# Layer 2 of a graph network: rows picked by TensorE for one column in eight, one chunk at a time, or in batches of four columns with a bfloat16 one-hot matrix

## What is computed

```python
k = (feats @ Wk + bk).reshape(n, H, D)
v = (feats @ Wv + bv).reshape(n, H, D)
score = jnp.sum(k[src] * q[dst], axis=-1)
score = jnp.exp(jnp.clip(score / SCALE, -5.0, 5.0))
wv = jax.ops.segment_sum(v[src] * score[..., None], dst, num_segments=n)
z = jax.ops.segment_sum(score, dst, num_segments=n)
wv = wv / (z[..., None] + 1.0)
```

## Time and profile before

| what | us |
|---|---|
| median of 3 runs | 6179.44 |
| lowest and highest | 6165.42, 6182.65 |
| span of the profiled execution | 5335.3 |
| median less span | 844.1 |
| busy in the span: DVE, POOL, PE, ACT | 3848.7, 3702.3, 3329.0, 2006.2 |
| edge stage of layer 2, first gather to last scan's start | 3097.36 to 4045.84 |

### The profile page before, as it was taken

How to read it: one execution, slowest core, us unless ns; L and a number is a source line. 1 busy time by engine, 2 the same in 40 slices (tenths; PEclk the granted TensorE clock), 3 DMA queues, 4 the chain that set the end, 5 groups by cost and what they waited for, 6 DMA issues and landing times. The chain is left out here.

```text
span 5335.3 us, 59849 instructions
## 1 busy us (share of the span) xinstructions
PE 3329.0 (62%) x17449; PEld 2791.6 (52%) x17449; DVE 3848.7 (72%) x5210; ACT 2006.2 (38%) x3469; POOL 3702.3 (69%) x3472
## 2 busy tenths in 40 slices
PE   1777777753999999999999467777674700000001
PEld 0444444432888889988888467666673500000001
DVE  3888888874999999999999569999996522222223
ACT  0666666641344444444444223333332311111111
POOL 4777777764788888888887356766774077777774
PEclk8899999986999999999999679999996955555555
DMA  7777777764888888888887333333332922222221
GB/s 292 247 267 255 262 264 263 257 214 146 309 319 319 319 321 321 320 320 321 320 321 282 89 92 110 108 108 108 109 108 64 382 52 55 53 54 53 54 56 43
DMA packets 390718, 1060.91 MB, mean 199 GB/s; under 512 B 138843, under 2 KB 161943, under 8 KB 349241
## 3 DMA queue, kind: packets, MB, share of 16 engines
q1 hardware_dynamic: 229430, 755.21, 37.7%
q0 software_dynamic: 104704, 161.21, 12.0%
q10 hardware_dynamic: 56448, 142.93, 7.1%
HBM read 667.35 MB, written 391.75 MB: 199 GB/s over the span
## 5 line engine op out<-in xcount | busy, mean ns | idle before, releaser
L1458 PE MATMUL COLS<-CF,XF 128*128 128x256 f32 x6272 | 1485.4, 380 | 5.6 <-DVE XF L1566 5.6
L1458 PEld LDWEIGHTS COLS<-CF,XF 128*128 128x128 f32 x6272 | 1134.6, 190 | 129.3 <-DVE XF L1566 6.0
L909 ACT ACTIVATE OUT<-SC 128x576 f32<-128x576 f32 (+3 forms) x392 | 574.9, 1467 | 1346.3 <-DVE SC L846 989.8
L784 POOL DMA_INDIRECT G<-rel_tab,IDX_rel x784 | 739.6, 943 | 390.5 <-issue 249.1
L1425 POOL DMA_INDIRECT G<-x_tab,SRC x784 | 833.2, 1063 | 231.5 <-issue 219.2
L784 POOL DMA_INDIRECT G<-xl_tab,IDX_src x784 | 749.7, 956 | 275.0 <-issue 264.4
L784 POOL DMA_INDIRECT G<-kv_tab,IDX_src x686 | 647.1, 943 | 298.3 <-issue 221.6
L1785 PE MATMUL CP<-IDENT,LROW 128*68 128x128 f32 (+1 forms) x12 | 3.4, 422 | 1049.9 <-DVE SM L1906 1049.9
L838 DVE TENSOR_TENSOR MSG<-G,EW 128x512 f32<-128x512 f32 x98 | 100.0, 1020 | 733.3 <-DMA G<-rel_tab,IDX_rel 724.7
L1785 PEld LDWEIGHTS CP<-IDENT,LROW 128*68 128x68 f32 (+1 forms) x12 | 1.5, 157 | 1051.3 <-DVE SM L1906 1051.2
L1196 PE MATMUL PICK<-KV,HOT 125*128 125x128 f32 x2548 | 364.3, 309 | 204.6 <-ACT G L1215 202.5
(11 more groups left out here) (274 smaller groups left out, 6907.6 us busy)
## 6 DMA issues: line engine op xcount, KB each, us to landing
SHB<-ea9t SPq DMA_DIRECT2D x196, 1024.0 KB
wkv_tab<-WKV SPq DMA_DIRECT2D x98, 1024.0 KB
WKV<-wkv_tab SPq DMA_DIRECT2D x98, 1024.0 KB, 5.9
scan<-OUT ACTq DMA_DIRECT2D x196, 288.0 KB
scan<-OUT ACTq DMA_DIRECT2D x98, 576.0 KB
rel_tab<-YS SPq DMA_DIRECT2D x25, 2048.0 KB, 7.3
RAW<-spread SPq DMA_DIRECT2D x196, 256.0 KB
spread_q<-ZQ SPq DMA_DIRECT2D x98, 512.0 KB, 5.3
```

Of the source, the lines that this page charges most:

```text
L784: pool.indirect_dma_start(out=self.G[g][b][:, c, :], out_offset=None, in_=tab, in_offset=bass.IndirectOffsetOnAxis(ap=self.IDX[which][b][: ...
L909: nc.scalar.activation(self.OUT[b][:, :, 0:WD], SC[b][:, 0:WD, 1:1 + C].rearrange("p r j -> p j r"), ACT.Copy).then_inc(self.copied_out, 1)
L1458: nc.tensor.matmul(acc, XF[b][:, k, edges_], CF[:, k, :], start=(k == 0), stop=False)
```

## The change

Layer 2 alone changes. Chunks 0 and 1 are gathered whole. From chunk 2 on, three chunks form a group in which TensorE picks 1, 1 and 2 columns (`picks`), so POOL gathers 7, 7 and 6, and the four picked columns are one batch of 512 edges. There are 32 batches.

- The source numbers of a batch come from the host already in a row (`src4`). SP loads them spread over all partitions into SRC4, ACT narrows them to 16 bits (ID16).
- DVE compares them in 25 instructions for a batch, one for each k: `tensor_scalar` with the partition's node number NODE_F[:, k] as scalar, 512 columns of uint16 in, bfloat16 out, into HOT, which is doubled. The 25 are cut into bursts of 6, 6, 6 and 7 and placed between ARG and MSG of each chunk, and one burst behind the scan.
- The table stays in SBUF as three bfloat16 pieces whose sum is the float32 value (KV3), made in the projection: ACT makes the first piece from TAB, DVE subtracts it (REST), ACT makes the second, DVE subtracts again into the third.
- PE multiplies with the roles turned round: KV3 is the weight and HOT the moving operand, 3 x 25 matmuls of 512 columns for a batch into PICK. The result is transposed, so ACT copies it out (`take`, TURNED), PE transposes it back in four parts (BACK) and ACT places the columns into G (`place`).
- KV's load at the start of the stage, the index loads of each chunk, SPREAD and SRC_F are gone; POOL takes its indices from SRC, which is loaded once. POOL's and DVE's chunks are written out.

```diff
+PICK_FROM = 2
+BATCHES = (NCH - PICK_FROM) // 3
+def picks(t):
+    return 0 if t < PICK_FROM else 2 if (t - PICK_FROM) % 3 == 2 else 1
...
+                        if pieces is not None:
+                            act.wait_ge(m_copied, len(units))
+                            nc.scalar.activation(KV3[:, :, 0, :], TAB[:, :, 0:128], ACT.Copy).then_inc(kv_high, 1)
...
+                                if pieces is not None and g == 1:
+                                    act.wait_ge(kv_rest, 1)
+                                    nc.scalar.activation(KV3[:, :, 1, :], REST[:, :, :], ACT.Copy).then_inc(kv_middle, 1)
...
+                            v.wait_ge(kv_high, 1)
+                            nc.vector.tensor_tensor(REST[:, :, :], TAB[:, :, 0:128], KV3[:, :, 0, :], ALU.subtract)\
+                              .then_inc(kv_rest, 1)
...
+                                if pieces is not None and g == 2:
+                                    v.wait_ge(kv_middle, 1)
+                                    nc.vector.tensor_tensor(KV3[:, :, 2, :], REST[:, :, :], KV3[:, :, 1, :],
+                                                            ALU.subtract).then_inc(kv_low, 1)
...
                     @block.gpsimd
-                        e.gathers(pool)
+                        wait(pool, src_in, 16)
+                        def step(t, n, b, first, last):
+                            wait(pool, e.scanned, t - 1)
+                            for c in range(C - picks(t)):
+                                pool.indirect_dma_start(
+                                    out=e.G[0][b][:, c, :], out_offset=None, in_=kv_tab,
+                                    in_offset=bass.IndirectOffsetOnAxis(ap=SRC[:, t * C + c:t * C + c + 1], axis=0),
+                                ).then_inc(e.rows_in[0][b], 16)
+                        all_chunks(step)
...
                     @block.tensor
+                        for i in range(BATCHES):
+                            wait(pe, compared, 4 * i + 4)
+                            wait(pe, taken, i)
+                            for piece in range(3):
+                                for k in range(K):
+                                    ins = nc.tensor.matmul(PICK[:, :], KV3[N, k, piece, :], HOT[i % 2][N, k, :],
+                                                           start=(piece == 0 and k == 0), stop=(piece == 2 and k == K - 1))
+                            ins.then_inc(picked, 1)
+                            wait(pe, taken, i + 1)
+                            wait(pe, placed, 3 * i)
+                            for q in range(4):
+                                ins = nc.tensor.transpose(BACK[:, q * P:(q + 1) * P], TURNED[:, q * P:(q + 1) * P],
+                                                          IDENT[:, :])
+                            ins.then_inc(turned_back, 1)
...
                     @block.scalar
+                        def narrow(i):
+                            wait(act, src4_in[i % 2], (i // 2 + 1) * 16)
+                            wait(act, compared, 4 * (i - 1))
+                            nc.scalar.activation(ID16[i % 2][:, :], SRC4[i % 2][:, :], ACT.Copy).then_inc(narrowed, 1)
+                        def take(i):
+                            wait(act, picked, i + 1)
+                            wait(act, turned_back, i)
+                            nc.scalar.activation(TURNED[:, :], PICK[:, :], ACT.Copy).then_inc(taken, 1)
...
                     @block.vector
+                        def compare(i, q):
+                            wait(v, narrowed, i + 1)
+                            wait(v, picked, i - 1)
+                            for k in range(6 * q, 6 * q + 6 if q < 3 else K):
+                                ins = nc.vector.tensor_scalar(HOT[i % 2][N, k, :], ID16[i % 2][N, :], NODE_F[N, k:k + 1],
+                                                              None, ALU.is_equal)
+                            ins.then_inc(compared, 1)
...
                         def step(t, n, b, first, last):
+                            if t < PICK_FROM:
+                                ahead = [(1, 2 * t), (1, 2 * t + 1)]
+                            else:
+                                i, r = divmod(t - PICK_FROM, 3)
+                                ahead = [(i + 2, q) for q in ((0, 1), (2,), (3,))[r] if i + 2 < BATCHES]
                             e.expand(v, t, n, b, first)
...
                             scores(t, n, b, first)
-                            if more:
-                                compare(t + 2, 0)
+                            if ahead:
+                                compare(*ahead[0])
                             e.sums(v, t, n, b, first, e.G[0][b][:, :, 64:128])
-                            if more:
-                                compare(t + 2, 1)
-                        chunks(v, step)
+                            if ahead[1:]:
+                                compare(*ahead[1])
+                        all_chunks(step)
```

More of the change, by code:

```diff
@@ L781, in step @@
                     pool.sem_inc(parked, 1)
-                    for c in range(self.gathered):
+                    for c in range(C):
                         for g, (tab, _, which) in enumerate(self.tables):
@@ L1210, in _ @@
+                        narrow(0)
+                        narrow(1)
                         wait(act, e.ready, e.N_READY)
-                        def place(t, b):
-                            wait(act, picked, t + 1)
-                            wait(act, e.scanned, t - 1)
-                            nc.scalar.activation(e.G[0][b][:, C - 1, :], PICK[:, 0:128], ACT.Copy).then_inc(placed, 1)
                         def step(t, n, b, first, last):
```

134 lines of the change are left out of this document (63 added, 71 removed).

## The result

| | before | changed |
|---|---|---|
| median, us | 6172.4 (6162.6 to 6182.7, 4 runs) | 5917.1 (5889.2 to 5942.1, 4 runs) |
| span of the profiled execution | 5335.3 | 5887.5, of a run of 5889.2 |
| ratio of the times | | 0.9587, 95% interval 0.9553 to 0.9622 |

The kernel became 255 us faster. The prediction had 82 us, 6097, with a range of 6058 to 6210: right in sign, wrong in size, and the time fell out of the range. One execution of an experiment stands apart, for a reason that is not known: 13670 us at a granted clock of 0.52, where the nine others of that kernel (before, with PE in a loop) on that chip took 5332 to 5342.

The account below looks back on a forecast made before the run. POOL's gathers were to bound layer 2's edge stage at 26.25 us per three chunks, saving 85 us; less 3 for the projection, 5335.3 - 82 + 844.1 = 6097 us, range 6058 to 6210.

Parts of the forecast that it names:

- what lies around it: Time outside the profiled span: 844.1 us, taken as unchanged and added to the forecast.
- The low end of my range: POOL's floor in layer 2: comparisons near XI's cost, no wait or hold, 24.98 us a period, 6058 us.
- something unseen: Catch-all case, sharing a chance of 0.04 with PE being late.
- The sum itself: Whole kernel: 85 us off layer 2's edge stage, less 3 for the projection, so 82 us off.
- POOL bounds the stage: Layer 2 edge stage: 20 gathers, 24.98 us, set the three-chunk period; 26.25 us with scan wait and holds.
- The hold by the shared access: Layer 2: comparisons delay POOL gather starts by about 0.1 us a burst, 0.4 us in three chunks.
- shut-out rival: Layer 2: gathers stand still while comparisons run, even mid-gather; 6258 or 6209 us; chance 0.13.
- burst-hold rival: Layer 2: a gather waits for its whole burst, 0.6 to 0.8 us each; 6152 us; chance 0.14.
- The wait for the scan: Layer 2: POOL waits 0.87 us for DVE's scan once in three chunks, after a six-gather chunk.
- The projection: Ahead of layer 2's edge stage: added ACT copies and DVE subtractions cost 3 us, bounds 0 and 13.6.
- rival of 1.2 GHz throughout: Layer 2: PE stays at 1.2 GHz, 31 us a batch; 6313 us; within 0.04 for PE late or something unseen.
- ACT's cover: Layer 2: ACT's extra work, under 1 us a chunk, fits its 3.2 us a chunk of waiting for ARG.

Follow-up runs that it names:

- b_unlinked_2: Kernel before with nobody waiting for TensorE in layer 2, its 25 matmuls a chunk kept; late chip: 6344.4 us beside 6169.2 for before.
- a_unlinked_2: Changed kernel with batch matmuls kept but their result untaken (no transposes, takes or placements); late chip: 5894.8 us beside 6169.2 for before.

## Why the prediction was wrong, step by step

**The step that failed** is the term "what lies around it, 6179.4 - 5335.3 = 844.1 by the median (830 to 847 by the three runs), I leave as it is". Of a timed run under 3 us lie around its span. The profile was of an execution without late starts (on quick chips before takes 5332 to 5346 us), the timed runs were on chips with them. Of the 255 us, 106 are what the change saves on a quick chip. The other 149 are late time that it happened to take away, 109 to 143 of them in layer 2 by the stages' lengths: that stage is 305 us longer on a late chip with the kernel before, and 162 to 196 with the changed one. The low end of my range, 6058, carried the same constant, and so could not hold the time. The prediction named it under what would make it wrong ("if the time around the span moves") but gave it no chance of its own beyond the 0.04 for "something unseen"; a difference of 16% between span and time deserved a rival. That the error fell on the side of the gain is luck: no term of the sum knew of late time.

Part of the mechanism of the extra gain is shown. In the kernel before each chunk has DVE wait for PE's spread and for PICK, so that each late start of PE goes through DVE's row, 280 us of waiting in 47 pieces, to POOL. In the changed kernel DVE's comparisons wait for the batch two before. That a kernel with nobody waiting for PE had a stage of 978 us shows that this link carried 256 of the 305. In the changed kernel another of the prediction's signs of being wrong came up on late chips: ACT does wait for PICK (132.9 us in 18 times), and through it DVE. But taking that link away left 989 us, so it is not what bounds the stage there; DVE's late scans are a part of it (76.4 of the 149 us that are left). Why engines start late at all stays open.

**The sum itself**, 85 us from the stage, less 3, measured on a quick chip: 102 us from the stage and 4 outside it, so 24 too few. One period of three chunks there, DVE, the rows that answer to the earlier trace rows (the last one begins the next period):

```profile
3498.24 1.90 DVE L1292 TENSOR_SCALAR HOT<-ID,NODE_F 125x512 bf16<-125x512 uint16 x6
3500.06 1.02 DVE L867 TENSOR_TENSOR MSG<-G,XE 128x512 f32<-128x512 f32 x1
...
3505.78 2.10 DVE L1292 TENSOR_SCALAR HOT<-ID,NODE_F 125x512 bf16<-125x512 uint16 x7
3507.80 1.03 DVE L867 TENSOR_TENSOR MSG<-G,XE 128x512 f32<-128x512 f32 x1
...
3512.99 0.69 DVE L1306 TENSOR_TENSOR T<-G,XE 128x512 f32<-128x512 f32 x1 [1.04 <-DMA G<-kv_tab,SRC]
...
3514.52 1.93 DVE L1292 TENSOR_SCALAR HOT<-ID,NODE_F 125x512 bf16<-125x512 uint16 x6
3516.37 1.03 DVE L867 TENSOR_TENSOR MSG<-G,XE 128x512 f32<-128x512 f32 x1
...
3518.90 1.82 DVE L1292 TENSOR_SCALAR HOT<-ID,NODE_F 125x512 bf16<-125x512 uint16 x6
3520.64 0.22 DVE L800 COPY XI<-XE 128x64 f32<-128x64 f32 x1
...
3523.83 1.89 DVE L1292 TENSOR_SCALAR HOT<-ID,NODE_F 125x512 bf16<-125x512 uint16 x6
```

and POOL's gathers in that stage (group), its one wait in three chunks, and the last gather, which answer to the earlier trace rows:

```profile
L1223 POOL DMA_INDIRECT G<-kv_tab,SRC x654 | 618.8, 946 | 220.3 <-issue 193.1 <-DVE SC L885 27.2
```
```profile
3501.06 0.94 POOL L1223 DMA_INDIRECT G<-kv_tab,SRC  x1 [0.30 <-issue]
3502.82 0.94 POOL L1223 DMA_INDIRECT G<-kv_tab,SRC  x1 [0.81 <-DVE SC L885]
...
3937.60 0.94 POOL L1223 DMA_INDIRECT G<-kv_tab,SRC  x1 [0.30 <-issue]
```

- *DVE.* The bursts take 1.82, 2.02, 1.85 and 1.74 us, together 7.43 against my 6.25: 0.30 a comparison, not 0.25. Undisturbed they start 0.26 apart, so the pitch itself was nearly right; the rest is that gathers hold them, some 0.85 us a period (763 comparisons last 0.380 on average, the median 0.346). The rest of three chunks takes 17.1 (25.59 less 7.43 and the idle 1.04) against 17.28. DVE needs 24.6 us where I had 23.5; the 31.9 us period of the double comparison (17.1 + 14.9) agrees. DVE keeps one spare microsecond in a period. I had left out that gathers hold comparisons, and it is hidden anyway.
- *POOL bounds the stage*: right. From the first gather's start to the last one's it is 840.4 us: less the first 20 and with one pitch of 1.25 added, 25.7 us a period, against 26.25.
- *The hold by the shared access*, 0.4 us a period on POOL: not there. The mean gather is 946 ns. Only three of the 640 behind the first 20 us took over 970. The shut-out rival and the burst-hold rival, 0.27 of the chance together, are both refuted, by the group row above and by the double comparison. The hold is on the other engine, as above: a comparison in a gather's middle lasts 0.53 us instead of 0.35. The rule of the Trainium skill on the shared port (SBUF — State Buffer, SBUF: two separate sides) has both sides: of a DVE instruction of certain kinds and a GpSimd one, whichever starts first keeps the other out for its whole length. These rows agree in so far as a gather makes a comparison wait. They do not in that a comparison beside a gather's first 0.4 us is not held, and in that gathers that start during a comparison still take 0.94 us. Why the instructions of the earlier trace rows did, stays open.
- *The wait for the scan*: the mechanism was right, once in three chunks, mostly 0.5 us over the usual 0.30 and 0.65 on average, where I had 0.87. In 32 periods the missing hold is 13 us and the shorter wait 7. Against that stand the 1.7 that I had taken off for the last two periods and 1 for the gathers' pitch of 1.251 instead of 1.249. That leaves the 17 us by which the stage beat my 85; with the 3 of the projection and the 4 outside they are the missing 24.
- *The projection*, +3: on a quick chip the first gather starts at 3097.21 after the change, against 3097.36. It costs nothing.
- *PE and ACT*: PE makes the 75 matmuls of a batch in 18.89 us, 0.25 each, between my two levels (first row): the granted clock is 0.50 in its first 3 us and 0.96 from 3512 to 3525, so the rival of 1.2 GHz throughout is refuted. ACT's cover, 310.7 us of waiting for ARG in the earlier trace rows, shrank to 216.8 and held (second row); ACT waits for PICK once, 4.2 us:

```profile
3507.93 18.89 PE L1236 MATMUL PICK<-HOT,KV 125*128 125x512 bf16 x75
```
```profile
ACT XE L923 <- DVE ARG L1314: 216.8, 96, 4.1
```

By these terms, a timed run on a quick chip would have been predicted at 5258 (5340.4 less 82) and measured at 5235.

## What to carry to other kernels

Compare the span of a profile with the times of the runs before anything else. If they differ, here by 16%, ask for a profile of an execution like the timed ones; failing that, give a chance of its own to the case that the missing time is inside, in the stages whose engines wait for each other in every step. A picked or computed result that is needed in each step passes on every late start of the engine that makes it; asked for two batches ahead it passed on less here (162 to 196 us instead of 305). And a part of a gain that comes from such a condition isn't there on the next chip: this change is worth 2.0% on one kind and 4.1% on the other.

## What the runs showed of the hardware that I had not expected

- Chips of one type differed by 15 to 17% on one program: the kernel before took 5332 to 5346 us on three chips and 6151 to 6274 on three. Single instructions of DVE and POOL last the same (in layer 2 a scan 1428 ns on either, a gather 943 and 946); PE's matmuls are longer (309 and 359 ns in the first half of a pick), at a lower granted clock. The difference is in starts that nothing in the profile explains. It hits layer 0 (+348 to +452 us of 1024), layer 2 (+305 of 943, with PE's loop +320) and layer 3, where PE does nothing (+83 of 989), and hardly layer 1 (+33 to +39 of 1623). Yet in layer 1 PE starts more instructions than in layer 2, and DMA moves four times as much (kernel before, late chip, layers 1 and 2; columns as above):

```profile
1700.00:3300.00 1600.00, 1581.36 (x8321) 1410.98 (x8320) 1465.77 (x1884) 656.48 (x1129) 1243.88 (x944) 1.00 0.83 313
3550.00:4700.00 1150.00, 755.30 (x4705) 712.39 (x4705) 823.64 (x816) 327.68 (x635) 600.04 (x635) 0.79 0.28 81
```

- While other engines work, PE on a late chip can sink to one instruction in 1.4 us, 12 matmuls in 30 us instead of 154 (30 over a whole stage), and does 272 as soon as they have ended. The late starts keep a step: in b_unlinked_2 neighbouring late starts of PE and its weight loads (over 0.5 us idle ahead, less than 4.5 us from one to the next) are 0.7, 1.4 or 2.1 us apart, to 0.05 us, in 665 of 671 cases, and in a_unlinked_2 in all 317. Of the changed kernel's late scans on DVE 77 of 80 begin with one of these starts. PE is late in a loop as well as written out. Why, is open: the number of instructions, the traffic of semaphores and the recording of the profile (every run here was recorded) weren't told apart.
- A tensor_scalar with a scalar per partition, uint16 in, bfloat16 out, 512 columns, starts every 0.26 us in a burst. Beside gathers it is 0.30 on average, since a comparison that meets the middle of a gather lasts 0.5 us and ends some 0.1 us behind it, while the gathers stay at 943 to 946 ns, with 50 comparisons in 32 us too.
